# A transformer layer on one core: h and the residual kept in PSUM, row normalisation on ScalarE, the router in thirteen pieces, and keys' norms applied as a scale of the tanh

## The reference

```python
mod = (silu(c) @ wmod).reshape(8, 6, 1, 256)      # sa, ca, ga, sb, cb, gb
h = layernorm(x) * (1 + ca) + sa
q, k, v = h @ wq, h @ wk, h @ wv                  # 16 query heads, 4 key/value heads of 128
q, k = rope(q), rope(k)
q = q / (norm(q) + 1e-6) * query_scale            # norm over the 128 values of a head
k = k / (norm(k) + 1e-6) * key_scale
scores = tanh((q @ k.T) / sqrt(128) / 50) * 50    # masked where |i - j| > 128
x = x + ga * ((softmax(scores) @ v) @ wo)
h = layernorm(x) * (1 + cb) + sb
weights = router(h @ Wr)                          # 8 per row; zone test, top 2 as fallback
out = sum over e of weights[e] * ((silu(h @ Wg[e]) * (h @ Wu[e])) @ Wd[e])   # F = 256
x = x + gb * out          # experts 0 and 1 have low-rank additions to Wg, Wu, Wd
```

## Time and profile before

| | us |
|---|---|
| median of 3 runs | 857.5 (856.58 to 857.96) |
| the profiled execution | 857.05 |
| its span, first to last instruction | 854.8 |
| TensorE busy | 807.0 (94%) |
| VectorE busy | 583.0 (68%) |
| GpSimd busy | 403.8 (47%) |
| ScalarE busy | 388.6 (45%) |

### The profile page before, as it was taken

The page is one execution under the profiler, slowest core; times in us unless marked ns, Lnnn a source line. Parts: engine busy times, 40 slices in busy tenths (PEclk is TensorE's granted clock), DMA queues, the critical chain, the costliest instruction groups (busy, mean ns, idle before and its releaser), DMA issues. The chain is left out here.

```text
span 854.8 us, 14160 instructions
## 1 busy us (share of the span) xinstructions
PE 807.0 (94%) x5118; PEld 712.3 (83%) x5118; DVE 583.0 (68%) x1193; ACT 388.6 (45%) x599; POOL 403.8 (47%) x525
## 2 busy tenths in 40 slices
PE   8889999999999899998899999899999999999997
PEld 7678988888888788887797898789878888888886
DVE  4688677478578867668868748776786454545577
ACT  3565655455554455555455556453323333323321
POOL 2787676567467557566647747310010100101380
PEclk8999999999999999999999999999999999999999
DMA  8200000000000000000000000020401101100002
GB/s 323 88 26 8 25 26 1 2 7 1 1 8 2 1 1 7 1 2 6 1 2 7 2 1 1 1 75 2 124 0 38 38 2 38 38 1 1 1 1 99
DMA packets 8019, 21.48 MB, mean 25 GB/s; under 512 B 1544, under 2 KB 4232, under 8 KB 7824
## 3 DMA queue, kind: packets, MB, share of 16 engines
q1 hardware_dynamic: 7376, 20.31, 7.0%
q10 hardware_dynamic: 576, 0.28, 0.1%
HBM read 18.47 MB, written 2.11 MB: 24 GB/s over the span
## 5 line engine op out<-in xcount | busy, mean ns | idle before, releaser
L581 PE MATMUL ps_o<-vaug,probs 128*128 128x129 f32 x1024 | 136.3, 276 | 9.6 <-DVE o_rows L1061 7.5
L581 PEld LDWEIGHTS ps_o<-vaug,probs 128*128 128x128 f32 x1024 | 127.9, 191 | 20.0 <-issue 13.2
L1349 POOL TENSOR_TENSOR root<-ssq,powers 128x4 f32<-128x4 f32 x80 | 83.3, 1041 | 100.6 <-DVE ssq L1029 100.6
L839 ACT ACTIVATE ps_s<-ps_s 128x1024 f32<-128x1024 f32 x64 | 64.5, 1008 | 123.9 <-PE ps_s L477 123.9
L1380 POOL TENSOR_TENSOR we_lo<-raw_e,we_hi 128x512 fp32r<-128x512 f32 x24 | 30.7, 1303 | 183.2 <-ACT we_hi L881 183.2
L1057 DVE RECIPROCAL rden<-ps_o 128x2 f32<-128x2 f32 x128 | 21.6, 169 | 136.7 <-PE ps_o L581 136.2
L1360 POOL TENSOR_TENSOR prod<-prod 128x512 f32<-128x512 f32 x80 | 102.9, 1287 | 0.0
L1032 DVE TENSOR_TENSOR prod<-ps_proj,cs 128x1024 f32<-128x1024 f32 x80 | 97.1, 1214 | 0.0
L1365 POOL TENSOR_TENSOR rows<-prod,rnorm 128x512 f32<-128x512 f32 x80 | 89.3, 1117 | 14.5 <-issue 7.8
L475 PE MATMUL ps_proj<-w_hi,h_hi 128*128 128x512 f32 x192 | 83.5, 435 | 9.6 <-DVE h_lo L1016 8.8
L477 PE MATMUL ps_proj<-w_hi,h_lo 128*128 128x512 f32 x192 | 75.8, 395 | 0.0
(11 more groups left out here) (172 smaller groups left out, 2161.0 us busy)
## 6 DMA issues: line engine op xcount, KB each, us to landing
raw_e<-in_we SPq DMA_DIRECT2D x8, 768.0 KB, 4.2
raw_p<-in_wqkv SPq DMA_DIRECT2D x6, 512.0 KB, 7.6
raw_e<-in_wo SPq DMA_DIRECT2D x4, 512.0 KB, 12.4
x_all<-in_x SPq DMA_DIRECT2D x1, 1792.0 KB, 7.6
out<-acc SPq DMA_DIRECT2D x3, 512.0 KB, 2.6
x_all<-in_wmod SPq DMA_DIRECT2D x1, 1024.0 KB, 10.0
gates_a<-gate_rows_dram SPq DMA_DIRECT2D x8, 128.0 KB, 2.9
gates_b<-gate_rows_dram SPq DMA_DIRECT2D x1, 1024.0 KB, 8.0
```

Of the source, the lines that this page charges most:

```text
L581: mm = pe.matmul(ps_o[:, h * (D + 1):(h + 1) * (D + 1)], probs[:, s % 2, at:at + P], vaug[b % 2][:, k, i // 2, :], start=(h == 0 and k == ...
L839: act.activation(ps_s[:], ps_s[:], ACT.Tanh).then_inc(tanh_done, 1)
L1349: pool.tensor_tensor(root[:, n % 2, :], ssq[:, n % 2, :], powers[:, 0:4], ALU.pow).then_inc(root_ready, 1)
```

## The change

What it does, part by part:

- **h in PSUM.** ScalarE scales and shifts the transposed rows in place in `ps_turn` and not into `hf`; `h_hi` and `h_lo` are read from there. `turn_h`, and with it the ScalarE work, moves from the middle of slot 2 to its end; `turn_h2` moves from slot 5 to 6 and the logits from 6 to 7.
- **Normalised rows by ScalarE.** `norm_rows` and `second_rows` become two activations of 128x256 each with scale 1/std and bias -mean/std; GpSimd makes the bias with two more small instructions. The very first rows stay with VectorE.
- **Residual in PSUM.** The gated output is written in place in `ps_y` and added to `x_all` at once, at the start of slot 2; the statistics stay at its end.
- **The router** in 13 pieces, one per slot and placed between the two halves of `normalise`. For the last four tiles they lie between the experts' products, and their second pair of exps comes after the first silu of the last kind.
- **Keys' norms.** The rotated keys are stored without division by their norm; the inverse norm goes into `knorm` and is the per-partition scale of the tanh. A tanh now covers one block of 128 keys, so there are two of 512 columns in place of one of 1024.
- **The first loads.** x is the first transfer of SP's queue; the identity matrix goes to ScalarE's queue; the first weight block's `hi` is copied by VectorE; `keep_busy` counts are 12, 6 and 4 for 8, 3 and 8; slot -2 comes ahead of the second part of the modulation.
- **The ends.** Two of the first expert's three `we_lo` blocks are made by VectorE (`split_first`). For 12 of the last 16 row tiles the final addition moves to GpSimd (`last_part`), two tiles at a time.

```diff
-SLOT_ROUTE = {ROUTE_FROM[g] + at: (g, n) for g in range(LATE) for n, at in enumerate((0, 2, 4, 5, 6))}
-LATE_ROUTE = {NEXT + 1: [0], NEXT + 2: [1, 2, 3, 4]}
+SLOT_ROUTE = {ROUTE_FROM[g] + at: [(g, n)] for g in range(LATE - 1) for n, at in enumerate((0, 2, 3, 5, 6, 7, 8, 9, 10, 11, 12, 13, 14))}
+LATE_ROUTE = {2 * NEXT + 3: [0], 2 * NEXT + 4: [1, 2], 2 * NEXT + 5: [3, 4], 2 * NEXT + 6: [5, 6, 7], 2 * NEXT + 7: [8, 9, 10, 11, 12]}
+LATE_ROUTE_EXP = {NEXT + 2: 0, NEXT + 3: 1}
...
+        here += [("r", b, r) for b, r in turns_of(s)]
         here += [("h", s // SLOTS + 1)] if turns_h(s) else []
-        here += [("r", b, r) for b, r in turns_of(s)]
-        here += [("h2", second(s, 5))] if second(s, 5) is not None else []
-        here += [("l", second(s, 6))] if second(s, 6) is not None else []
+        here += [("h2", second(s, 6))] if second(s, 6) is not None else []
+        here += [("l", second(s, 7))] if second(s, 7) is not None else []
...
+            sp.dma_start(x_all[:, 0:TT, :], a["x"][:, 0:TT, :]).then_inc(x_in[0], 16)
             sp.dma_start(wmod_sb[:, :, 0:2 * E], a["wmod"][:, :, 0:2 * E]).then_inc(wmod_in[0], 16)
...
-            keep_busy(8)
+            keep_busy(12)
...
-            keep_busy(3)
             turn_h(0)
-            keep_busy(8)
+            keep_busy(6)
             slot(FIRST)
+            keep_busy(4)
+            slot(FIRST + 1)
             pe.wait_ge(wmod_in[1], 16)
...
-                    act.activation(hf[:, k, :], ps_turn[:, bank, k * S:(k + 1) * S], ACT.Identity,
+                    part_of = ps_turn[:, bank, k * S:(k + 1) * S]
+                    act.activation(part_of, part_of, ACT.Identity,
                                    bias=modc[:, b, k:k + 1], scale=modc[:, b, 2 + k:3 + k]).then_inc(h_mod, 1)
+            def norm_rows(b):
+                act.wait_ge(ln_rstd, b + 1)
+                act.wait_ge(h_turned, b)
+                if b > 2:
+                    act.wait_ge(h2_turned, b - 2)
+                for t in range(TT):
+                    act.activation(xn[:, t, :], x_all[:, TT * b + t, :], ACT.Identity,
+                                   bias=shift[:, t:t + 1], scale=rstd[:, t:t + 1]).then_inc(ln_done, 1)
...
-                act.activation(ps_s[:], ps_s[:], ACT.Tanh).then_inc(tanh_done, 1)
+                if i == 0:
+                    act.wait_ge(rnorm_ready, NR * b + TT)
+                for t in range(TT):
+                    act.activation(ps_s[:, t, :], ps_s[:, t, :], ACT.Tanh,
+                                   scale=knorm[:, b % 2, t, i // 2:i // 2 + 1]).then_inc(tanh_done, 1)
...
+                if m in LATE_ROUTE_EXP:
+                    route(LATE, LATE_ROUTE_EXP[m])
...
-                dve.tensor_tensor(ygated[:], ps_y[:].rearrange("p (t e) -> p t e", t=TT), ga, ALU.mult).then_inc(y_gated, 1)
+                dve.tensor_tensor(y, y, ga, ALU.mult).then_inc(y_gated, 1)
                 dve.wait_ge(y_gated, b + 1)
-                dve.tensor_tensor(xb, xb, ygated[:], ALU.add).then_inc(x_updated, 1)
+                dve.tensor_tensor(xb, y, xb, ALU.add).then_inc(x_updated, 1)
...
+            def split_first(m3):
+                sl = slice(2 * m3, 2 * m3 + 2)
+                dve.wait_ge(we_hi_done, m3 + 1)
+                dve.tensor_tensor(we_lo[0][:, sl, :], raw_e[:, 0, sl, :], we_hi[0][:, sl, :], ALU.subtract).then_inc(we_first, 1)
...
+                for g, piece in SLOT_ROUTE.get(s, ()):
+                    route(g, piece)
                 if live(s - 1):
                     normalise(s - 1, 1)
...
+                if PROJ[p][0] == "k":
+                    if n >= RING:
+                        pool.wait_ge(rope_turned, n + 1 - RING)
+                    pool.tensor_tensor(rows[:, n % RING].rearrange("p h (a d) -> p h a d", a=2), whole, turned, ALU.add).then_inc(rows_ready, 1)
+                    return
...
+            def last_part(n):
+                for half in range(2):
+                    d = 2 * (len(TILES) - 4 + n) + half
+                    sl = slice(2 * half, 2 * half + 2)
+                    pool.wait_ge(acc_done, 2 * d + 2)
+                    pool.wait_ge(base_done, 2 * n + half + 1)
+                    pool.tensor_tensor(acc[n][:, sl, :], acc[n][:, sl, :], part[:, half], ALU.add).then_inc(final_add, 1)
```

More of the change, by code:

```diff
@@ L218, in build @@
         mv = sb("mv", [P, TT, 2])
-        veps = sb("veps", [P, TT])
-        rstd = sb("rstd", [P, TT])
+        first = sb("first", [P, 4, TT])
+        veps, rstd, minus, shift = (first[:, n, :] for n in range(4))
+        shift2 = sb("shift2", [P, NT])
         ssq = sb("ssq", [P, 2, 4])
@@ L703, in slot @@
                     turn_rows(bb, r)
-                if (b2 := second(s, 5)) is not None:
+                if turns_h(s):
+                    turn_h(s // SLOTS + 1)
+                if (b2 := second(s, 6)) is not None:
                     turn_h2(b2)
-                if (b2 := second(s, 6)) is not None:
+                if (b2 := second(s, 7)) is not None:
                     router_logits(b2)
@@ L736, in _ @@
             mm.then_inc(mod_rows, 1)
-            pe.wait_ge(mod_ready, 2)
-            for s in range(FIRST + 1, LAST + 1):
+            for s in range(FIRST + 2, LAST + 1):
                 if s <= 0:
@@ L974, in _ @@
                 mid_head(2 * m + 1)
-                for stage in LATE_ROUTE.get(m, ()):
-                    if stage < 2:
-                        route(LATE, stage)
                 for e, m3 in EXPERT_STEPS.get(m, ()):
@@ L1177, in _, with route @@
             count = [0]
-            def route(g, stage):
+            def route(g, piece):
                 gt, eq = r_gt[max(g - 1, 0)], r_eq[max(g - 1, 0)]
@@ L1193, in route @@
                 fb_e = r_fb[:].unsqueeze(3).broadcast_to([P, 4, NE, NE])
-                if stage == 0:
+                if piece == 0:
                     dve.wait_ge(small_in, 48)
@@ L1267, in slot @@
                     h_tail(b + 1)
+                if i == 2 and 1 <= b <= B:
+                    statistics(b - 1)
                 if i == 3 and b >= 1:
@@ L1273, in slot @@
                     product(g)
+                for e, m3 in SLOT_EXPERT.get(s, ()):
+                    if (e, m3) in ((0, 0), (0, 1)):
+                        split_first(m3)
                 for b2 in SLOT_H2.get(s, ()):
@@ L1306, in _ @@
                 product(2 * m)
-                if m == NEXT:
-                    second_rows(B - 1)
+                for piece in LATE_ROUTE.get(2 * m, ()):
+                    route(LATE, piece)
                 product(2 * m + 1)
@@ L1314, in _ @@
                     read_logits(B - 1)
+                if m == NEXT + 3:
+                    for piece in LATE_ROUTE.get(2 * m + 1, ()):
+                        route(LATE, piece)
                 accumulate(2 * m - 2)
@@ L1318, in _ @@
                     fold(i)
-                for stage in LATE_ROUTE.get(m, ()):
-                    route(LATE, stage)
+                if m != NEXT + 3:
+                    for piece in LATE_ROUTE.get(2 * m + 1, ()):
+                        route(LATE, piece)
             accumulate(2 * len(TILES) - 2)
@@ L1428, in _ @@
                     split_e(e, m3)
-            for n in range(4):
+            for n in range(LATE):
                 rest_of_output(n)
+            rest_of_output(LATE)
+            for n in range(LATE):
+                last_part(n)
 def tables():
```

192 lines of the change are left out of this document (112 added, 80 removed).

## The result

The changed kernel takes **818.8 us** (median of 4 runs, 818.31 to 819.95) against 857.5 (856.58 to 857.96, 4 runs): ratio 0.9552, 95% interval 0.9536 to 0.9569. Forecast were 820 and a range of 812 to 836. The span of the profiled execution is 817.3, the very figure of the sum (redone, 854.8 - 37.6 is 817.2).

The account below looks back on a forecast made before the run. TensorE, busy 807.0 of 854.8 us, was taken as the bound, leaving its 47.8 us idle and what pauses cost beside. Terms summed to 40.6 us, less 3 given back: 820 us, range 812 to 836.

Parts of the forecast that it names:

- xn, 6.0 us: TensorE's waits for xn before turn_h: seven go, with 0.25 us more for each, 6.0 us.
- h_lo, 10.3 us: Projection in slot 3: all six waits for h_lo go, 8.8 us plus 0.25 each, 10.3 us.
- rival B: VectorE's queue behind takes half of the batch terms; about 835 us, between 828 and 846; chance 0.23.
- Second transposition, 6.6: Moved from slot 5 to 6, its six waits for kT_lo go: 5.1 us plus 0.25 each, 6.6 us.
- Router, 6.4: o_rows waits after router stages and slot 4's xn go, 7.4 us; pieces may stick out, so 6.4 taken.
- Rival C: Slower: router pieces ahead of the second normalise all stick out in 33 slots; about 865 us; chance 0.03.
- Two tanhs, nothing: ScalarE between scores and exp: two tanhs take 12 us more in all, taken as covered; uncovered up to 12.
- First expert, 3.9: Wait for the first we_lo and half-clock stretch behind it, 5.4 us in all; 3.9 taken, 1.5 left.
- Last router, 2.5: The wait for mid at 641.61, 2.75 us, goes despite two more table loads; 2.5 us taken.
- The start, 4.4: Before the first scores: 2.1 us from two key rotations and 2.3 from earlier loads, together 4.4 us.
- The 3 us given back: Subtracted for waits opened by the new bank order and longer chains, 0.4 us in each of 8 batches.
- The end, 0.5: Four additions leave VectorE's last chain, 1.7 us, but the last down must be awaited; 0.5 us taken.

Follow-up runs that it names:

- a_xn_dve: The changed kernel with both kinds of normalised rows (norm_rows, second_rows) made by VectorE again at their old places; 825.4 us, ratio 0.9626.
- f_keys_pool: The changed kernel with GpSimd dividing the keys' rows by their norms again and one tanh of 1024 columns per slot; 825.8 us, ratio 0.9627.
- d_stages: The changed kernel with the router of the first 12 row tiles in five stages at slots' ends again; 824.7 us, ratio 0.9621.
- m_sum_last: The changed kernel with batches 0 to 6's gated output in SBUF, added to x_all behind h_lo and ahead of the statistics; 821.7 us, ratio 0.9589.
- l_hlo_first: The kernel before with only h_lo moved ahead of the addition to x_all and its statistics in slot 2; 859.7 us, ratio 1.0033.

## Why the prediction was right, point by point

- **What bounds it, and the per-batch waits.** Right. Body by body the change brought 34.3 us; my terms behind the start were 33.2 (36.2 less 3). The two lists of waits agree: 27.0 us of waits went whole in 28 places, with 0.25 behind each 7.0, two got 2.4 shorter in all, the clock gave 1.7, and three new ones take 2.7. That makes 35.4. Batches without router work were to be 3.5 us shorter or more, and are 3.9 shorter.
- **xn, 6.0 us.** The wait is gone, as forecast. I named both the rows from ScalarE and the later place, and either alone would have removed it. The 4.9 us that a_xn_dve gave back are not this term, since none of its waits is for `xn`; they are VectorE's time, paid at `o_rows`. That they lie near 6.0 is luck.
- **h_lo, 10.3 us.** The mechanism is shown: with the addition and the statistics ahead of it the waits return (7.4 us, body 8.9), with `turn_h` in the middle others come (body 6.1), and the order alone is worth 6.5 in the changed kernel. Whether both had to be out of the way no run shows. The kernel before with the order alone is no faster: there the queue behind paid, which was my rival B, and the clock on top. What held B off is the place of `turn_h`, VectorE's shorter queue, or both; no run separates these.
- **Second transposition, 6.6.** Measured 6.8. `turn_o` does not wait for `qT_lo` in the batches, as reckoned.
- **Router, 6.4.** Measured 5.0 for the pieces of three groups, about 6.7 without what they cost the first expert. Rival C is answered: only in slot 58 does a wait stand behind pieces. The one wait that I left standing, behind the gates' values, stands: 1.69 at 80.43.
- **Two tanhs, nothing.** Body 784.3 either way, within 0.8 us (f_keys_pool). They take ScalarE 15 us and not the 12 that I reckoned.
- **First expert, 3.9.** Right: the wait fell from 3.45 to 1.49, and the stretch at half clock, 1.7 us, is gone, 3.7 together. Against GpSimd in the changed kernel it measured 5.0, since there the wait is 3.9 and the clock takes 2.7. The rest of 1.5 was taken from another wait by likeness; d_stages shows that here it is the router's pieces.
- **Last router, 2.5.** The wait is gone, and five table loads stand in the trace. ScalarE, after:

```profile
597.93 0.60 ACT L926 ACTIVATE silu<-ps_s 128x512 f32<-128x512 f32 x1 [1.03 <-PE ps_s L489]
598.54 1.28 ACT L941 ACT_TABLE_LOAD   x1
599.84 0.23 ACT L941 ACTIVATE r_w<-r_c 128x32 f32<-128x32 f32 x1
...
600.20 1.28 ACT L926 ACT_TABLE_LOAD   x1
601.50 0.60 ACT L926 ACTIVATE silu<-ps_proj 128x512 f32<-128x512 f32 x1
```

  From the first silu's end to the exp it is 1.3 us, the load and nothing more. The Trainium skill (ScalarE: Activation LUTs, What ACT_TABLE_LOAD costs) has a drain beside the load and about 2.66 us for both; no drain is to be seen here, and the row was the better price.
- **The start, 4.4.** Here the working failed, by its terms and by what it left out. Measured were 3.2 in the first execution. The 2.3 us for the loads are 0.54 in the one pair of like executions: I followed x and `powers`, and not `wmod`, which was put behind x in the same queue. The 2.1 for the keys are there on GpSimd (2.55), but with them undone the first scores are 3.5 us later or more, by the clock. And GpSimd is no longer last: its rows end at 28.65 and the first scores come 4.35 us later, where it was 2.54. The last transposition waits for nobody but stands in TensorE's queue behind a projection, and VectorE has `ssq` and `prod` ahead of `qT_lo`:

```profile
30.53 0.69 DVE L1070 TENSOR_REDUCE ssq<-sq 128x4 f32<-128x512 f32 x1 [0.70 <-ACT sq L838]
...
31.14 1.22 DVE L1073 TENSOR_TENSOR prod<-ps_proj,cs 128x1024 f32<-128x1024 f32 x1
...
32.27 0.68 DVE L1098 TENSOR_TENSOR qT_lo<-ps_turn,qT_hi 128x512 fp32r<-128x512 f32 x1
33.00 0.50 PE L487 MATMUL ps_s<-qT_hi,kT_hi 128*128 128x512 f32 x1 [1.86 <-DVE qT_lo L1098]
```

  What the new order of slot -2 and the idle matmuls do to the start was not run by itself. And two executions of one kernel gave 3.2 us and -0.1 for this term, by the clock; I had no row on how much the start scatters. That the span came out at 817.3 is luck: an error of 1.2 here against one of 1.1 in the body.
- **The 3 us given back.** Near in size, not in kind: not 0.4 us in each batch, but three new waits that come once, 0.77, 0.32 and 0.89 us, with 0.25 behind each 2.7. The one of 0.89 comes from the addition at the slot's start: in m_sum_last, without it there, 0.16 is left.
- **The end, 0.5.** The last wait for `part` went from 0.6 to 0.2. From the start of TensorE's last matmul to the end of the span it is no shorter, 4.7 us (812.62 to 817.3) where it was 4.5 (850.27 to 854.8). Nor did `last_part` make it 1.3 us longer, the other end that I had given. It was not run by itself.

## What to carry to other kernels

A wait names the tile that is late, not the cause: before moving its instruction up in a full queue, ask who is behind it. Here that alone moved 8 us from one name to another; it paid only in the changed kernel, where `turn_h` is later and VectorE's queue shorter. And before calling an instruction slow, look at what it then takes: moved by less than a microsecond, the same addition took 0.87 us and not 1.44. When one load is put first, follow those it pushes back, too. And when an edit's effect is as small as the scatter of the start, compare from a fixed event behind the start instead of the total.

## What the runs showed that was not expected

- The changed kernel's start has TensorE at 1.2 GHz for stretches whose number and length change between executions (0.80 and 0.50 granted in 10 to 15; 1.00 and 0.66 in 25 to 30). The first scores came 3.3 us apart.
- Where this start set the pace less, it didn't scatter so: in the kernel before and in l_hlo_first the first scores come at 36.16 and 36.02, with TensorE at 1.2 GHz from 8 to 16 us in the one and not in the other.
- The length of a wait alone doesn't tell whether the clock falls behind it. It was at 0.56 for 3.4 us behind one wait of 2.62 us and at 1.00 behind another (l_hlo_first). It fell behind the wait of 2.53 us for `mid` there and behind one of 1.84, and not behind that of 2.51 in the kernel before. Behind 3.9 us it was 0.50 for 4 us and 0.83 for the next 4; behind 1.49 us (after, the first expert) it stayed at 1.00.
- The same VectorE instruction with two operands in SBUF took 0.78 us in one place and 1.42 in another, beside GpSimd, though against TensorE its start was moved by only 0.6 us.
